# Multi-query layer: keys projected and loaded ahead of the queries, and bursts of two to four score pairs

## What is computed

```python
def _L0_attn_ref(x, w_q, w_k, w_v, w_out, softmax_scale):
    q = (x @ w_q.T).reshape(B, S, 16, 16)      # 16 heads of 16
    k = x @ w_k.T                              # one key head for all: [B, S, 16]
    v = x @ w_v.T
    scores = jnp.einsum('bshd,btd->bhst', q, k) * softmax_scale[0]
    attn = jax.nn.softmax(scores, axis=-1)
    out = jnp.einsum('bhst,btd->bshd', attn, v).reshape(B, S, D)
    return out @ w_out.T

x = x + _L0_attn_ref(_layernorm(x), ...)
x = x + _L0_ffn_ref(_layernorm(x), ...)        # 256 -> 256, input and kernel rounded to fp8
```

## Time and profile before

| | |
|---|---|
| median of 3 runs | 4020.94 us (4015.92 to 4025.86) |
| the profiled execution, its own time | 4027.29 us |
| its span, first to last instruction | 4025.4 us |
| first layer, last store issued | 2024.5 us after the start |
| mean granted PE clock, of full speed | 0.958 |
| PE, DVE, ACT, POOL busy over the span | 93%, 73%, 62%, 43% |

### The profile page before, as it was taken

How to read it: one execution, slowest core, us unless ns; L and a number is a source line. 1 busy time by engine, 2 the same in 40 slices (tenths; PEclk the granted TensorE clock), 3 DMA queues, 4 the chain that set the end, 5 groups by cost and what they waited for, 6 DMA issues and landing times. The chain is left out here.

```text
span 4025.4 us, 76045 instructions
## 1 busy us (share of the span) xinstructions
PE 3736.8 (93%) x25352; PEld 1890.3 (47%) x25352; DVE 2940.5 (73%) x8436; ACT 2513.7 (62%) x5347; POOL 1722.8 (43%) x1956
## 2 busy tenths in 40 slices
PE   6999999999999999999649999999999999999998
PEld 2344444444444444444214555555555555555554
DVE  5888888888888888888227777776777777777664
ACT  2777777777777777777415555555555555555554
POOL 1255445455554554544533443443343344344331
PEclk7999999999999999999759999999999999999999
DMA  3333333334333333343046656755755765665570
GB/s 67 70 69 75 81 68 82 80 64 86 77 70 79 76 80 70 75 85 60 26 84 111 115 104 100 122 104 94 126 106 94 118 112 104 102 119 104 95 122 28
DMA packets 323077, 352.93 MB, mean 88 GB/s; under 512 B 28101, under 2 KB 277371, under 8 KB 322683
## 3 DMA queue, kind: packets, MB, share of 16 engines
q1 hardware_dynamic: 320641, 347.01, 46.3%
q10 hardware_dynamic: 2048, 1.05, 0.1%
HBM read 221.08 MB, written 117.44 MB: 84 GB/s over the span
## 5 line engine op out<-in xcount | busy, mean ns | idle before, releaser
L656 DVE TENSOR_REDUCE maxima<-ps_vector 128x1 f32<-128x512 f32 x2048 | 1282.2, 682 | 256.4 <-PE ps_vector L425 249.9
L1549 DVE CUSTOM_DVE_ANT_0 ps_max<-ps_max,mask 128x128 f32<-128x128 f32 (+3 forms) x2048 | 987.5, 508 | 533.6 <-PE ps_max L1248 513.6
L1406 ACT ACTIVATE probs<-ps_exp 128x512 f32<-128x512 f32 (+3 forms) x2048 | 823.0, 440 | 785.4 <-PE ps_exp L1267 717.4
L554 ACT ACTIVATE probs<-ps_scalar 128x512 f32<-128x512 f32 x2048 | 1082.8, 600 | 232.6 <-PE ps_scalar L439 226.4
L425 PE MATMUL ps_vector<-k_op,q_op 48*128 48x512 f32 x2048 | 737.6, 453 | 112.1 <-DMA k_op<-kparts 79.4
L439 PE MATMUL ps_scalar<-q_op,k_op 50*128 50x512 f32 x2048 | 727.9, 449 | 1.6 <-ACT probs L554 0.4
L1263 PE MATMUL ps_exp<-q_op,k_op 101*128 101x512 bf16 (+3 forms) x2048 | 614.8, 301 | 26.9 <-ACT probs L1406 17.8
L1248 PE MATMUL ps_max<-k_op,q_op 99*128 99x128 bf16 (+3 forms) x2048 | 619.6, 304 | 19.5 <-DMA k_op<-qk_parts 16.9
L425 PEld LDWEIGHTS ps_vector<-k_op,q_op 48*128 48x128 f32 x2048 | 345.0, 190 | 531.4 <-DVE maxima L656 293.3
L458 PE MATMUL ps_pv<-probs,v_op 128*32 128x512 f32 x4096 | 549.1, 608 | 0.5 <-ACT oT L566 0.5
L1694 POOL TENSOR_SCALAR neg_mean<-meanvar 128x4 f32<-128x4 f32 x64 | 12.6, 197 | 1088.4 <-issue 783.6
(11 more groups left out here) (127 smaller groups left out, 5221.9 us busy)
## 6 DMA issues: line engine op xcount, KB each, us to landing
q_op<-qk_parts SPq DMA_DIRECT2D x192, 256.0 KB, 5.4
qk_parts<-qparts SPq DMA_DIRECT2D x128, 384.0 KB, 3.1
q_op<-qk_parts SPq DMA_DIRECT2D x384, 128.0 KB, 6.4
k_op<-qk_parts SPq DMA_DIRECT2D x384, 128.0 KB, 6.8
qk_parts<-qparts SPq DMA_DIRECT2D x64, 512.0 KB, 3.8
xin<-in_x SPq DMA_DIRECT2D x32, 512.0 KB, 4.8
xres<-in_x SPq DMA_DIRECT2D x32, 512.0 KB, 4.5
x_mid<-xo SPq DMA_DIRECT2D x32, 512.0 KB, 3.2
```

Source lines behind the costliest of these rows:

```text
L554: act.activation(probs[:, quad % 2, at:at + S], ps_scalar[:, bank_of("scalar", "exp", p, 0, par), :], ACT.Exp).then_inc(ps_out["exp"], 1)
L656: dve.tensor_reduce(at, ps_vector[:, bank_of("vector", "max", k, d, par), :], AX.X, ALU.max).then_inc(ps_out["max"], 1)
L1406: act.activation(probs[:, quad % 2, at:at + nq], ps_exp[:, bank, 0:nq], ACT.Exp).then_inc(exp_done, 1)
L1549: ins = dve.tensor_tensor_reduce(row, row, mask[:, S - keys:S], 1.0, LOWEST, ALU.add, ALU.max, at)
```

## The change

It moves steps of the plan and of two queues; no computation is added or left out. The plan has 21 lines before and after, with 64 pairs and 16 `V`. Its bursts are now of two to four pairs (before: twenty of three and one of four). `kv` stands in the fourth line (before: the sixth) and `ont`, `otr`, `xt`, `ffn`, `stat1` and `stat2` stand at other places. On SP, `load_operands` is cut in two: `load_keys` issues the six key loads of both units and stands first, `load_queries` issues three query loads of one unit, and the maxima rows of quad 3 come ahead of the second `store_parts`. On POOL the key split moves ahead of the second LayerNorm.

```diff
 PLAN_MQA = """
-PPP   qk:0:1 stat2:2:-2 stat2:3:-2
-PPP V m:1:0 otr:2:-1
-PPP V ont:0:-1
+PPP stat2:2:-2 qk:0:1
+PPP otr:2:-1 V
+PPP m:1:0 V
+PPP stat2:3:-2 V kv:0:1 stat1:0:2
 PPP V
+PPPP split:2:0 V
+PPP ont:0:-1 otr:3:-1
+PP V m:2:0
+PP V exponent:0:-2
+PPP v:0:1 V ont:1:-1
+PPP qk:1:1
 PPP V
-PPP   split:2:0 kv:0:1 stat1:0:2
-PPP V m:2:0 otr:3:-1
+PPPP split:3:0 V
+PPP m:3:0 V
+PPPP otr:0:0 out:0:-1 ft:0:-2
 PPP V
-PPP V ont:1:-1 exponent:0:-2
-PPP V
-PPP   split:3:0 qk:1:1
-PPP V m:3:0 otr:0:0
-PPP V v:0:1
-PPP V
-PPP V ft:0:-2
-PPP   split:0:1 out:0:-1 stat1:1:2
-PPP   out:1:-1 stat1:2:2 stat1:3:2
-PPP V m:0:1 stat2:0:-1
-PPP V ffn:0:-2 otr:1:0
-PPP V xt:0:2 stat2:1:-1
-PPPP V ffn:1:-2 xt:1:2 split:1:1
+PPP split:0:1 stat1:1:2 out:1:-1
+PP ffn:0:-2 m:0:1 V ffn:1:-2 stat1:2:2 stat1:3:2 stat2:0:-1 stat2:1:-1
+PPP V otr:1:0
+PPP V xt:0:2 xt:1:2
+PPPP V split:1:1
 """
...
+            def load_keys(c, par):
+                if not valid(c):
+                    return
+                sp.wait_ge(kv_split, c + 1)
+                if due(seen := (c - 1) * HEADS * NT):
+                    sp.wait_ge(ps_full["exp"], seen)
+                for unit in range(2):
+                    for g in range(len(K_TERMS)):
+                        at = HALF_ROWS * unit + g * DH
+                        sp.dma_start(k_op[at:at + DH, par, :].bitcast(F32),
+                                     kparts[0:DH, par, K_TERMS[g], :].bitcast(F32)).then_inc(op_loaded[unit], 16)
+
-            def load_operands(c, par, unit):
+            def load_queries(c, par, unit):
...
-                if unit == 0:
-                    sp.wait_ge(kv_split, c + 1)
                 for g in range(len(Q_TERMS)):
                     at = HALF_ROWS * unit + g * DH
                     src = qk_dram[par, Q_TERMS[g], unit, :, :]
                     sp.dma_start(q_op[at:at + DH, par, :, :].bitcast(F32),
                                  src.rearrange("(h d) s -> d h s", d=DH)).then_inc(op_loaded[unit], 16)
-                    sp.dma_start(k_op[at:at + DH, par, :].bitcast(F32),
-                                 kparts[0:DH, par, K_TERMS[g], :].bitcast(F32)).then_inc(op_loaded[unit], 16)
...
                 store_parts(b + 1, 1 - par, 0)
-                load_operands(b + 1, 1 - par, 0)
+                load_keys(b + 1, 1 - par)
+                load_queries(b + 1, 1 - par, 0)
                 load_maxima(b, par, 2)
+                load_maxima(b, par, 3)
                 store_parts(b + 1, 1 - par, 1)
-                load_maxima(b, par, 3)
-                load_operands(b + 1, 1 - par, 1)
+                load_queries(b + 1, 1 - par, 1)
...
             def body(b, par):
                 split_qk(b + 1, 0)
+                split_kv(b + 1, 1 - par)
                 normalise(1, b - 2, par)
                 over_s_in(b - 2)
-                split_kv(b + 1, 1 - par)
                 to_fp8(b - 2)
```

## The result

The changed kernel takes **3877.69 us** (median of 4 runs, 3863.94 to 3880.39) against 4018.43 us before (4 runs): a ratio of **0.9644**, with a 95% interval of 0.9626 to 0.9662. Forecast were 3872 us and faster. The profiled execution is the one of 3863.94 us, with a span of 3862.2 us and a mean granted clock of 0.977 (before: 4025.4 and 0.958). The last store of the first layer is issued at 1863.6 us instead of 2024.5, 160.9 of the 163.2 us between the two spans, so the gain lies in that layer. The profiled execution is the fastest of the four, 14 us under their median, so its bodies are somewhat shorter than those of a usual run: by the medians the gain is 140.7 us, or 4.5 us in each of 31 bodies.

A forecast was written before the change was run, and what follows sets the result against it. PE sets the pace, with 4.44 us a body lost to one operand wait and its slow clock. 59.33 - 4.4 - 0.8 + 0.35 = 54.5 us, -149 us over 31 bodies, gives 3872 us; range 3835 to 3950.

The forecast's parts named there:

- Operands: PE's wait at pair 33 for key and query loads goes, with its slow clock: -4.4 us a body, bounds -4.4 and -2.7.
- The walk from `kv` to pair 33: PE's steps timed through the new plan: `kv` starts at 9.3 us, pair 33 is due at 26.8.
- The margin: Time by which the queries land before pair 33 is due at 26.8 us: 0.9 us, or 0.1 at the upper bound.
- the wait shrinks but stays: Rival, chance 0.20: 1.2 us of pair 33's operand wait and 1.3 of slow clock stay; 57.0 us a body, 3949 us.
- Behind the loads: Maxima rows queued on SP: quad 2's costed at nothing, 0 to 0.7 us; quad 3's at nothing, bound 0.5.
- POOL: LayerNorm of b-2 behind the key split gives z at 19.4 us, `exponent` comes at 21.6; costs nothing.
- the cover's worth: The 2.2 us to spare between z from POOL and DVE's `exponent`; each further us of lateness costs one.
- Bursts: PE waiting for DVE's banks: +1.4 us for four bursts of four, other waits go, together -0.8; bounds -2.7 and +1.4.
- Sum: Body length: 59.33 - 4.4 - 0.8 + 0.35 = 54.5 us, -4.8 in each of 31 bodies, -149 us.
- + 0.35 for small residues: An allowance of 0.35 us a body, added in the sum for small residues.
- DVE's idle time: DVE's idle time before reduces was to fall from 7.1 to about 2.5 us a body.
- The rule on HBM bandwidth: Some 358 GB/s from HBM: query data in about 2.2 us instead of 6.2; the row's 131 GB/s was used instead.

The follow-up runs named there:

- e4: The changed kernel with `kv` alone put back, two lines later in the plan: 4080.64 us, ratio 1.0139.
- e6: The kernel before with half the bytes in each query load, the other heads' queries staying zero: 3902.63 us, ratio 0.9703.
- e1: The changed kernel with the old plan put back, keeping the new orders on SP and POOL: 4129.40 us, ratio 1.0265.
- e7: The changed kernel with bursts of three throughout (the last is four), other steps in their places: 3964.53 us, ratio 0.9855.
- e2: The changed kernel with the old orders on SP and POOL, so the new plan alone: 3947.14 us, ratio 0.9806.
- e9: The changed kernel with four of the five POOL instructions of `to_fp8` cut in halves: 3869.28 us, ratio 0.9618.
- e12: The changed kernel with all five POOL instructions of `to_fp8` in halves, the short fifth included: 3865.05 us, ratio 0.9626.
- e3: The changed kernel with the old SP order alone, POOL and plan as changed: 3870.99 us, ratio 0.9617.
- e10: The changed kernel with four of five `to_fp8` instructions in halves and the old SP order: 3894.75 us, ratio 0.9683.

## Why the prediction was right

The step that it rests on is right in size and cause. *Operands*: the wait at pair 33 and its slow clock went, and e4, e6 and e1 show that the loads behind `kv` made it. The walk from `kv` to pair 33 was right to 0.02 us. The walk's other lines are right to 0.1 us as well. The margin was put at 0.9 to 0.1 and was the lower: the waits of the kernel after have PE's weight loads waiting for queries in 22 bodies, 0.8 us each, PE itself in four. The rival *the wait shrinks but stays* was near, and e7 is that case, with pair 33 due a little earlier. In four bodies some 0.2 us of the wait stayed. In the prediction's sum a wait costs its own length and some slow clock; these cost some 3 us each, through the split.

*Behind the loads* and *POOL*: right. Maxima rows of quad 2 cost nothing, and DVE never waits for z; the cover's worth is in e4.

*Bursts*: the term of -0.8 is not borne out. Start to start in the body of 730.60, the four bursts of four take 1.71 us each, 0.59 over a free one, so three more of them are +1.8 and not +1.4; all bursts together take 2.6 us more than free ones, and in the body before from 914.86 they took 2.5 besides the operand wait. What was gained elsewhere just paid for the bursts of four. (The rows of idle time show less of this, 0.5 us a body between e7 and the kernel after, since a tile that starts late may leave PE busy with the last one.) In return the steps between the bursts take some 0.9 us less than in the body before, most of it at `m`, which the prediction had left as they were. This compares one body with one.

*Sum*: 54.5 as predicted, by luck in part, since errors cancel. Undisturbed bodies take about 53.8 us, 0.7 less than forecast, though 0.35 of residues had been added. The six long ones bring the mean up by as much. The step that missed is "+ 0.35 for small residues": it had no cause, and the cause was the split of quad 3, which the prediction costed at nothing. The trace of before had a hold of up to 2.36 us in three bodies, but `m` came 3 us behind the end of the split there, with `qk` between them. The new plan took that cover away, and the walk through it had no line for DVE's split. That was the thing late next.

*DVE's idle time* before reduces is 4.0 us a body, not 2.5. 3.1 us went from there, and another 1.7 from before the reciprocals, which waited 43.9 / 25.3 us for `otr` in the kernel before and wait for nothing now (line 724 above). Together it is the 4.8 us of the body; the prediction had all but 0.2 us from the reduces.

*The rule on HBM bandwidth* (the Trainium skill, "DMA: Bandwidth & Descriptors", section "Where 436 GB/s comes from") would have left a wide margin. The queries arrive just when due, which speaks for the 131 GB/s of the earlier trace rows.

**What stays open.** Runs of the changed kernel differ by 16 us (3863.94 to 3880.39). The number of long bodies would do it, since each costs some 3 us, but only one execution was profiled. The 0.2 us of operand wait that decide in most cases whether a body is long were read from traces and not varied by themselves. A kernel with `split:3` right behind pair 32, or with another step between it and `m`, was not run; it is the change that these traces ask for next.

## What to carry to other kernels

Where one step heads a chain of engine, split, load and use, move it by the chain's length and not by its own place in the plan: `kv` two lines later costs 203 us, and the reordered queues help only with it there. When steps move, ask what stood between a producer and its consumer, and covered a delay: here `qk` between the split and `m`. When a large wait goes, ask which short instruction on the path was late behind it, and what long instruction on the neighbouring engine can meet it. Cut those long instructions (or place them) before the new order is tuned to 0.2 us, as a plan that is right for one queue order was 76 us off with another.

## What the runs showed of the hardware

A DVE instruction that reads and writes SBUF, of 128x16 elements, takes 0.19 us in the median of the kernel after, and up to 2.1 us when it starts while POOL is at work on SBUF. In e2, e9 and the kernel after it ends 0.02 to 0.04 us after the POOL instruction, and it gets short as that gets short (2.13 and 1.04 us; in e12 0.62). The split of another quad is held in 28 bodies of the kernel after, and takes 0.55 to 0.69 us until a POOL instruction of 1.16 ends; PE doesn't wait for it. Not every POOL instruction holds: during line 789 (128x256, float32 to bf16, 0.55 us) the split's instructions take 0.16 to 0.19 and 0.25 to 0.27 us. DVE's reduces from PSUM keep their 0.68 us throughout (at most 0.69). The Trainium skill ("SBUF — State Buffer", section "SBUF: two separate sides") says that DVE and GpSimd share a port pair under an exclusive lock, held for the whole instruction, for DVE operations of some kinds. By this rule the held one waits to the end of the other; the traces agree, and the halving (42.0 to 3.6 us of waits) is what it would give. No run here tells which kinds of operation are held.

Two rows of maxima land 1.84 us after the issue of the second with nothing large ahead of them (quad 3 in the kernel after, by the updates of their semaphore in the trace), 2.07 right behind the store in e3 and e10, and 4.8 to 6.4 behind the three query loads (quad 2 in the kernel after). The Trainium skill ("DMA: Bandwidth & Descriptors", section "Two DMAs through the same engine are not ordered") has descriptors of a queue start in order, and the rows behind the query loads agree. The store itself delays the rows by only 0.2 us: it is SP's wait in front of it that makes them late.
